# Transformer layer, attention part: a rotating accumulator bank, and row-maximum units made of every sixteenth query

## Chip, core and metric

One Trainium2 chip, one of its cores. The metric is the device time of one execution in microseconds (us): the median of the runs, for the kernel before 504.43 us.

## What is computed

A pre-norm layer on 1024 tokens of width 512 in which attention and feed-forward run side by side on the same normalized input: 32 query heads of dimension 16 share 8 key/value heads, all projections use binarized weights.

```python
def _L0_attn_ref(hidden_states, q_weight, q_scale, k_weight, k_scale, v_weight, v_scale, o_weight, o_scale):
    ...
    q = bitnet_linear(hidden_states, q_weight, q_scale)
    ...
    k = jnp.repeat(k, N_REP, axis=1)
    v = jnp.repeat(v, N_REP, axis=1)
    scores = jnp.einsum('bhqd,bhkd->bhqk', q, k) / np.sqrt(HEAD_DIM)
    attn = jax.nn.softmax(scores, axis=-1)
    out = jnp.einsum('bhqk,bhkd->bhqd', attn, v)
    out = out.transpose(0, 2, 1, 3).reshape(b, s, HIDDEN)
    return bitnet_linear(out, o_weight, o_scale)
...
xn = _layernorm(x, axis=-1)
x = x + _L0_attn_ref(xn, ...) + _L0_ffn_ref(xn, ...)
```

## The kernel before

The kernel has four stages. **Opening** (to about 60 us): loads, layer norm, transposition of x, signs of the weights, the first projections. **Feed-forward** (to 152.8 us): 28 steps F0 to F27 of gate and up matmuls, with the rest of the projections and the first 32 row units (A0 to A31) strewn between them. **Attention** (152.8 to 460 us). **Tail**: down projection, output projection, sums. The order on TensorE, VectorE and ScalarE in the second stage is written out by hand as three strings (`pe_order`, `dve_order`, `act_order`).

**Blocks and steps.** Attention runs over 16 blocks, one for each of the 8 key heads g and each half `hf` of the queries (512 of 1024). A block has 8 steps, one for each tile of 128 keys, so there are 128 steps. A block's queries are 4 heads (REP) times 512. In one step and for each of the 4 heads, TensorE makes a tile of scores [128 keys x 512 queries] into a PSUM bank, ScalarE takes its exponential into SBUF (`probs`), and TensorE multiplies that with the values of the step before (`times_values`, in two halves of 256 queries, four heads side by side in strips of 32 columns of the array) into an accumulator bank. The value matrix has ones beside it, so the accumulator also holds the sums of the softmax.

**Row units.** The exponential needs each query's maximum. For it the scores are computed a second time, the other way up: a row unit takes 128 queries as the stationary operand and all 1024 keys as the moving one (`half_rows`, twice 512 keys, into a pair of banks out of 0 to 3), and VectorE reduces the pair to one negated maximum for each query (`row_max`, a column of `nmx` [128, 16]). 16 units make a block (UNITS); they are computed two blocks ahead, two in each step. The maxima then have to become two extra rows of the queries in `qst` (a high and a low fp16 part), so that the score matmul subtracts them: for that TensorE transposes `nmx` (`transpose_max`, step "T") to [16 units, 128 queries], ScalarE copies it out of PSUM with a scale (`take_max`), GpSimd splits it into two fp16 parts (`split_max`, `shp`), and SyncE copies each part to two rows of `qst` (`load_shift`, four DMAs a block).

**Banks.** Banks 0 to 3 are those of the row units, 4, 5 and 6 go round among the score tiles, and bank 7 is always the accumulator. The transposition takes one turn of the ring of three, in step 1 of each block (`T_STEP`), between the score tiles of steps 1 and 2. At the end of a block ScalarE copies bank 7 to `osb` (`take_output`), and the first values matmul of the next block waits for that copy (`pv_free`).

**Order in a step** (`scores`): score tile 0, half a row unit, score tile 1, the other half, values part 0 of the step before, score tile 2, both halves of the second row unit, score tile 3, values part 1. A score tile is in one half of the array's rows, the row unit beside it in the other, and the two run together. From step 108 on (LATE, `late_scores`) the last 8 row units and then 56 down-projection products a tile fill the steps; the first of these steps waits for the last row maximum, since it takes bank 3 for scores.

A unit's queries as the stationary operand (`half_rows`), and the wait for the accumulator's copy (`times_values`):

```python
                                        qst[low:low + KROWS, par, hf, head, qt * P:(qt + 1) * P],
...
                        pe.wait_ge(pv_free, gp * 4 + s // TT + 2)
```

Of the kernel before, what the change touches and what calls it, by code (L numbers as in the profile page):

```python
# [13 lines left out]
P = 128  # L14
# [13 lines left out]
def layer_kernel(nc, x, wq, wk, wv, wo, wq_rows, wk_rows, wv_rows, wo_rows, sq, sk, sv, so, gate, up, down, sg, su, sd, out,  # L28
# [32 lines left out]
                "A17 F20 T0 A18 A19 F21 A20 A21 F22 A22 A23 F23 A24 A25 F24 A26 A27 F25 A28 A29 F26 A30 A31 F27 ")  # L61
# [5 lines left out]
                 "F5 F6 X4 F7 F8 F9 F10 F11 X5 F12 F13 F14 F15 F16 Y0 F17 Y1 F18 F19 F20 T0 F21 F22 F23 F24 F25 F26 "  # L67
# [6 lines left out]
    T_AT = [n for kind, n in pe_order[:pe_order.index(("T", 0))] if kind == "F"][-1]  # L74
# [3 lines left out]
    assert T_AT % 2 == 0 and len(PROJ) == 6  # L78
    assert pe_order.index(("T", 0)) > pe_order.index(("A", UNITS - 1))
# [23 lines left out]
    T_STEP = 1  # L103
    BLOCK = TT * REP
# [6 lines left out]
    def entry(j, i):  # L111

        e = j * REP + i
        e += j > T_STEP
        return e

    def score_bank(e):
        return 4 + e % 3

    T_ENTRY = (T_STEP + 1) * REP  # L120
    assert (BLOCK + 1) % 3 == 0


    LATE_SCORES = [4, 5, 6, 3]
    LATE_T = 0
    LATE_T_STEP = 3
# [5 lines left out]
    assert LATE % TT > T_STEP and ROWS_END - 1 == (2 * NG - 2) * TT + LATE_T_STEP  # L132
    assert LATE + len(QUOTAS) == NG * STEPS and sum(QUOTAS) == len(FILLS) and sum(QUOTAS[:ROWS_END - LATE]) == 2 * FT

    def t_step(block_):

        return LATE_T_STEP if block_ == 2 * NG - 2 else T_STEP

# [5 lines left out]
    def bank_of(gp, s, i):  # L144

        if gp * 2 * STEPS + s >= LATE:
            return LATE_SCORES[i]
        return score_bank(entry(s % TT, i))

    def exps_before(e):  # L150

        return e - 2 if e - 3 < T_ENTRY else max(e - 3, T_ENTRY)

# [6 lines left out]
    with ExitStack() as ctx:  # L160
# [3 lines left out]
        def sem(name):  # L164
            return ctx.enter_context(nc.semaphore(name))
# [87 lines left out]
        shp = sb("shp", [UNITS, 2, 2, P], F16)  # L253
        mxs = sb("mxs", [UNITS, P], F32)
# [74 lines left out]
        maxT_ready = sem("maxT_ready")  # L329
        max_taken = sem("max_taken")  # L330
# [169 lines left out]
        def _(pool):  # L500
# [96 lines left out]
        def _(act):  # L597
# [20 lines left out]
            def take_max(v, bank):  # L618

                act.wait_ge(maxT_ready, v + 1)  # L620
                act.wait_ge(shift_ready, v)
                nc.scalar.activation(mxs[:, :], ps[0:UNITS, bank, 0:P], ACT.Copy, scale=1.0 / LIFT).then_inc(max_taken, 1)  # L622

            splits = 0
            for kind, n in act_order:
# [51 lines left out]
                elif kind == "T":  # L677
                    take_max(0, 6)
# [17 lines left out]
            def exps(gp, s, last):  # L696
# [3 lines left out]
                if j == t_step(step // TT) + 1 and not (last and s >= STEPS + TT):  # L700
                    take_max(gp * 4 + s // TT + 1, LATE_T if step >= LATE else score_bank(T_ENTRY))
                act.wait_ge(probs_free, step + 1)
                for i, r in enumerate(ROUND):
                    act.wait_ge(scores_ready, step * REP + i + 1)
                    nc.scalar.activation(probs[:, s % 2, r, :], ps[:, bank_of(gp, s, i), :], ACT.Exp,  # L705
# [4 lines left out]
            def take_output(gp, s):  # L710
# [5 lines left out]
                nc.scalar.copy(osb[:, hf, :], ps[:, 7, :]).then_inc(pv_free, 1)  # L716
# [31 lines left out]
        def _(dve):  # L748
# [205 lines left out]
            def step_rows(gp, s, last):  # L954
# [3 lines left out]
                ga_ = gp_ * 2 + par + 1  # L958
                if step < LATE:
# [27 lines left out]
            def down_out(i):  # L987
# [5 lines left out]
                bank = FILL_BANKS[i % 2] if i < FILL else i  # L993
# [47 lines left out]
        def _(pe):  # L1041
# [73 lines left out]
            def feed_forward(w, z):  # L1115
                f, hf = w // 2, w % 2
                if z == 0:
# [6 lines left out]
                    if w == T_AT + 1:  # L1124
                        pe.wait_ge(max_taken, 1)
# [9 lines left out]

            def half_rows(par, hf, idx, b):
# [265 lines left out]
```

## Time and profile before

| | |
|---|---|
| Times of three runs | 503.80, 504.43, 505.09 us (median 504.43) |
| Profiled execution, span | 502.6 us |
| TensorE busy | 479.6 us (95%) |
| VectorE busy | 417.2 us (83%) |
| ScalarE busy | 350.3 us (70%) |
| GpSimd busy | 94.4 us (19%) |
| Granted TensorE clock | 1.000 all through (its upper level, 2.4 GHz) |

The profiled execution's own time is its span, from the first to the last instruction; the device time of a run includes what lies around it, 1.8 us at the median. "PE" is TensorE's matmuls, "PEld" its weight loads, which run beside them; DVE is VectorE, ACT ScalarE, POOL GpSimd. Matmul ends are modelled, so a PE that shows as busy is not necessarily at its peak: what counts is the distance from one start to the next.

### The profile page before, as it was taken

The page shows a single profiled execution, that of the slowest core. Times are in us where ns is not written, and L with a number is a line of the kernel's source. Part 1 is how long each engine was busy: PE and PEld are TensorE (multiplying, and loading weights), DVE is VectorE, ACT ScalarE, POOL GpSimd, SP SyncE. Part 2 cuts the span into 40 slices and gives each one's busy share as a digit, 9 for nine tenths or more (in the row PEclk, how much of TensorE's full clock was granted, in tenths as well). Part 3 has the DMA queues.
Part 4 walks back from the last instruction along what each step waited for, and adds up shares of the span by engine and source line. Part 5 has one row for each costly group of instructions (what it writes and reads, how often), then busy time and mean ns, then how long its engine had stood idle before and what let it go on. Part 6 is the DMA issues. An engine that isn't in the chain of part 4 may idle for free.

```text
span 502.6 us, 10338 instructions
## 1 busy us (share of the span) xinstructions
PE 479.6 (95%) x4186; PEld 163.0 (32%) x4186; DVE 417.2 (83%) x487; ACT 350.3 (70%) x655; POOL 94.4 (19%) x138
## 2 busy tenths in 40 slices
PE   0899999999999999999999999999999999999996
PEld 0564444434332222222222222222222233333442
DVE  6879868676778999999999999999999955223986
ACT  1853643343229999999999999999999978874000
POOL 4212334534323000000000000000000113241021
PEclk9999999999999999999999999999999999999999
DMA  8862782641103802102102211111120034452321
GB/s 260 252 123 81 159 171 38 187 91 22 23 0 42 148 23 63 40 24 65 39 25 63 40 37 49 41 53 32 41 62 24 14 96 107 110 148 79 105 82 45
DMA packets 31302, 39.02 MB, mean 78 GB/s; under 512 B 6608, under 2 KB 20816, under 8 KB 31256
## 3 DMA queue, kind: packets, MB, share of 16 engines
q1 hardware_dynamic: 22232, 27.34, 19.0%
q0 software_dynamic: 8304, 10.95, 11.8%
q8 instruction: 33, 0.54, 0.5%
q10 hardware_dynamic: 720, 0.08, 0.1%
q14 instruction: 13, 0.11, 0.1%
HBM read 33.24 MB, written 10.35 MB: 87 GB/s over the span
## 4 chain that ended last, share of the span: by engine, by line
PE 86%; ACT 8%; DVE 3%; issue 1%; DMA 1%; SPq 0%; ACTq 0%; DVEq 0%
PE ps L1301 25%; PE ps L1131 19%; PE ps L1235 12%; PE ps L1140 8%; ACT room L705 6%; PE ps L1207 5%; PE ps L1194 5%; PE ps L1110 3%; PE ps L1335 3%; PE ps L1271 2%; ACT osb L716 1%; DMA hlo<-x 1%; DVE nmx L838 1%; PE ps L1048 1%; PE ps L1102 1%
## 5 line engine op out<-in xcount | busy, mean ns | idle before, releaser
L838 DVE TENSOR_REDUCE nmx<-ps 128x1 f32<-128x1024 f32 x248 | 284.6, 1216 | 14.5 <-PE ps L1140 14.2
L705 ACT ACTIVATE room<-ps 128x512 f32<-128x512 f32 x512 | 272.4, 598 | 20.9 <-PE ps L1271 11.0
L1301 PE MATMUL ps<-room,vcur 128*32 128x256 f32 (+1 forms) x1880 | 159.1, 410 | 4.3 <-ACT osb L716 4.1
L1140 PE MATMUL ps<-kA,qst 48*128 48x512 f16 x496 | 140.4, 382 | 0.0
L1235 PE MATMUL ps<-qst,kB 50*128 50x512 f16 x432 | 132.2, 382 | 0.8 <-DVE room L937 0.5
L1131 PE MATMUL ps<-room,wf 128*128 128x512 f16 x448 | 100.6, 379 | 0.0
L1301 PEld LDWEIGHTS ps<-room,vcur 128*32 128x32 f32 x1880 | 37.1, 108 | 100.8 <-issue 55.6
L686 ACT ACTIVATE room<-ps,gsc 128x512 f32<-128x512 f32 x28 | 19.2, 687 | 61.6 <-PE ps L1131 61.6
L1131 PEld LDWEIGHTS ps<-room,wf 128*128 128x128 f16 x448 | 42.4, 98 | 55.1 <-issue 7.2
L1235 PEld LDWEIGHTS ps<-qst,kB 50*128 50x128 f16 x432 | 26.8, 93 | 89.1 <-ACT room L705 79.8
L543 POOL TENSOR_TENSOR hlo<-room,hhi 128x512 f16<-128x512 f32 x28 | 34.1, 1217 | 87.4 <-ACT hhi L616 87.4
L549 POOL TENSOR_TENSOR shp<-mxs,ones 16x128 f16<-16x128 f32 x16 | 8.1, 508 | 224.3 <-ACT mxs L622 224.3
L937 DVE SCALAR_TENSOR_TENSOR room<-ps,usc,room 128x512 f32<-128x512 f32 x28 | 20.8, 744 | 13.9 <-issue 10.0
L1140 PEld LDWEIGHTS ps<-kA,qst 48*128 48x128 f16 x496 | 26.3, 94 | 7.5 <-issue 7.5
L1194 PE MATMUL ps<-wd,hhi 128*32 128x512 f16 x224 | 22.3, 379 | 0.0
L1194 PE MATMUL ps<-wd,hlo 128*32 128x512 f16 x224 | 22.3, 379 | 0.0
L1207 PE MATMUL ps<-wd,hhi 128*128 128x512 f16 x56 | 21.2, 379 | 0.0
L1207 PE MATMUL ps<-wd,hlo 128*128 128x512 f16 x56 | 21.2, 379 | 0.0
L616 ACT CAST hhi<-room 128x512 f16<-128x512 f32 x28 | 17.1, 611 | 1.0 <-DVE room L937 1.0
L1110 PE MATMUL ps<-room,sgn 128*128 128x512 f16 x80 | 17.8, 379 | 0.0
L509 POOL TENSOR_TENSOR room<-room,parts 128x512 f32<-128x512 f32 x7 | 9.5, 1363 | 39.0 <-DVE room L994 27.4
L978 DVE TENSOR_TENSOR y<-y,ga 128x1024 f32<-128x1024 f32 (+1 forms) x5 | 5.0, 998 | 14.1 <-DMA ga<-r_scratch 14.1
(136 smaller groups left out, 320.1 us busy)
## 6 DMA issues: line engine op xcount, KB each, us to landing
qst<-q_scratch SPq DMA_DIRECT2D x32, 192.0 KB, 3.6
o_scratch<-osb SPq DMA_DIRECT2D x16, 256.0 KB, 2.3
q_scratch<-parts SPq DMA_DIRECT2D x12, 256.0 KB
hlo<-x SPq DMA_DIRECT2D x8, 256.0 KB, 6.1
parts<-x POOLq DMA_DIRECT2D x8, 256.0 KB, 3.5
wf<-gate POOLq DMA_DIRECT2D x14, 128.0 KB, 3.9
wf<-up POOLq DMA_DIRECT2D x14, 128.0 KB, 6.0
wd<-down POOLq DMA_DIRECT2D x1, 1792.0 KB, 14.3
```

The lines of the kernel that those rows point to most:

```text
L543: nc.gpsimd.tensor_tensor(hlo[:, f, hf * HALF:(hf + 1) * HALF], hb[:, w % 2, :], hhi[:, f, hf * HALF:(hf + 1) * HALF], ALU.subtract).then_ ...
L686: nc.scalar.activation(gt[:, n % 2, :], ps[:, 4 + 2 * (n % 2), :], ACT.Silu, scale=gsc[:, f:f + 1]).then_inc(gt_ready, 1)
L705: nc.scalar.activation(probs[:, s % 2, r, :], ps[:, bank_of(gp, s, i), :], ACT.Exp, scale=gam_reg[par][r]).then_inc(scores_free, 1)
L838: nc.vector.tensor_reduce(nmx[:, hf, idx:idx + 1], bank_pair(idx % 2), AX.X, ALU.max, negate=True).then_inc(rows_free, 1)
L937: nc.vector.scalar_tensor_tensor(out=hb[:, n % 2, :], in0=ps[:, 5 + 2 * (n % 2), :], scalar=usc[:, f:f + 1], in1=gt[:, n % 2, :], op0=ALU. ...
L1110: mm = nc.tensor.matmul(ps[:, 2 * (n % 2) + hf, :], sgn[:, c, c0:c0 + P], xs[:, c, hf * HALF:(hf + 1) * HALF], start=(c == 0 and xs is xhi ...
L1131: mm = nc.tensor.matmul(ps[:, 4 + 2 * (w % 2) + z, :], wf[:, f % WF_BUFS, z, c * P:(c + 1) * P], xs[:, c, hf * HALF:(hf + 1) * HALF], star ...
L1140: return nc.tensor.matmul(ps[:, 2 * (idx % 2) + b, :], qst[low:low + KROWS, par, hf, head, qt * P:(qt + 1) * P], kA[low:low + KROWS, par, ...
L1194: mm = nc.tensor.matmul(ps[32 * c:32 * c + 32, FILL_BANKS[i % 2], :], (hhi, hlo)[part][:, f, lo:lo + 32], wd[:, f, :], start=(f == 0 and p ...
L1207: mm = nc.tensor.matmul(ps[:, i, :], (hhi, hlo)[part][:, f, i * P:(i + 1) * P], wd[:, f, :], start=(f == 0 and part == 0), stop=(f == FT - ...
L1235: nc.tensor.matmul(ps[:, score_bank(e), :], kB[low:low + SROWS, par, kt % (TT // 2) * P:(kt % (TT // 2) + 1) * P], qst[low:low + SROWS, pa ...
L1301: mm = nc.tensor.matmul(ps[32 * r:32 * r + 32, 7, of], vcur[:, par, key_tile(r, j), :], probs[:, s % 2, r, of], start=(j == 0 and part == ...
```

## The change

It has two parts. **The accumulator bank changes at each block**: at step 1 of a block, before score tile 2, the bank next in the ring becomes the block's accumulator, and the accumulator of the block before joins the ring in its place. So the first values matmul of a block no longer waits for ScalarE's copy; score tile 2 of that step does. **A row unit takes every sixteenth query** (all 4 heads, 32 queries of each, starting at query u for unit u) instead of 128 neighbours of one head. Then `nmx` [128, 16], read row by row, has the 2048 queries in their order, and needs no transposition. The T steps of TensorE and the `take_max` steps of ScalarE are gone; GpSimd scales `nmx` itself (twice, once to fp32 and once to fp16) and subtracts, and the DMAs read 128 partitions of 32 bytes in place of 16 of 256. VectorE gets one wait at the start of each block, that the maxima which it overwrites have been split.

```diff
-                "A17 F20 T0 A18 A19 F21 A20 A21 F22 A22 A23 F23 A24 A25 F24 A26 A27 F25 A28 A29 F26 A30 A31 F27 ")
+                "A17 F20 A18 A19 F21 A20 A21 F22 A22 A23 F23 A24 A25 F24 A26 A27 F25 A28 A29 F26 A30 A31 F27 ")
...
-                 "F5 F6 X4 F7 F8 F9 F10 F11 X5 F12 F13 F14 F15 F16 Y0 F17 Y1 F18 F19 F20 T0 F21 F22 F23 F24 F25 F26 "
+                 "F5 F6 X4 F7 F8 F9 F10 F11 X5 F12 F13 F14 F15 F16 Y0 F17 Y1 F18 F19 F20 F21 F22 F23 F24 F25 F26 "
...
+    SPLIT_AT = 20
+    ring, spare = [4, 5, 6], 7
+    score_banks, score_after, value_banks = {}, {}, [7]
+    last_exp, last_copy = {}, {}
+
+    for step in range(LATE):
+        block_, j = step // TT, step % TT
+        for i in range(REP):
+            if i == 2 and j == 1 and block_ >= 1:
+                value_banks.append(ring.pop(0))
+                ring.insert(0, spare)
+                last_copy[spare] = block_
+                spare = value_banks[-1]
+            bank = ring.pop(0)
+            ring.append(bank)
+            score_banks[step, i] = bank
+            score_after[step, i] = last_exp.get(bank, 0), last_copy.pop(bank, 0)
+            last_exp[bank] = step * REP + i + 1
...
-        shp = sb("shp", [UNITS, 2, 2, P], F16)
-        mxs = sb("mxs", [UNITS, P], F32)
+        shp = sb("shp", [P, 2, 2, UNITS], F16)
+        mxs = sb("mxs", [P, UNITS], F32)
...
             def split_max(v, hf):
-                pool.wait_ge(max_taken, v + 1)
-                nc.gpsimd.tensor_tensor(shp[:, hf, 0, :], mxs[:, :], ones[0:UNITS, :], ALU.mult).then_inc(shift_step, 1)
-                pool.wait_ge(shift_step, v + 1)
+                pool.wait_ge(rows_free, 2 + (v + 1) * UNITS)
+                pool.wait_ge(shift_ready, v)
+                nc.gpsimd.tensor_scalar(mxs[:, :], nmx[:, hf, :], 1.0 / LIFT, 1.0, ALU.mult, ALU.mult).then_inc(shift_step, 1)
+                nc.gpsimd.tensor_scalar(shp[:, hf, 0, :], nmx[:, hf, :], 1.0 / LIFT, 1.0, ALU.mult,
+                                        ALU.mult).then_inc(shift_step, 1)
+                pool.wait_ge(shift_step, 2 * (v + 1))
                 nc.gpsimd.tensor_tensor(shp[:, hf, 1, :], mxs[:, :], shp[:, hf, 0, :], ALU.subtract).then_inc(shift_ready, 1)
...
-                if w == T_AT + 1:
+                if w == SPLIT_AT:
                     split_max(0, 0)
...
-                nc.scalar.activation(mxs[:, :], ps[0:UNITS, bank, 0:P], ACT.Copy, scale=1.0 / LIFT).then_inc(max_taken, 1)
...
-                nc.scalar.copy(osb[:, hf, :], ps[:, 7, :]).then_inc(pv_free, 1)
+                nc.scalar.copy(osb[:, hf, :], ps[:, value_banks[v], :]).then_inc(pv_free, 1)
...
+                if j == 0 and step < LATE:
+                    dve.wait_ge(shift_ready, ga_ * 2 + hf - 1)
...
+            def unit_queries(low, par, hf, idx):
...
+                return qst[low:low + KROWS, par, hf].rearrange("p h (i u) -> p u h i", u=UNITS)[:, idx]
...
-                                        qst[low:low + KROWS, par, hf, head, qt * P:(qt + 1) * P],
+                return nc.tensor.matmul(ps[:, 2 * (idx % 2) + b, :], unit_queries(low, par, hf, idx),
...
-                nc.tensor.transpose(ps[0:UNITS, bank, 0:P], nmx[:, hf, :], ident[:, :]).then_inc(maxT_ready, 1)
...
-                    pe.wait_ge(scores_free, block_ * BLOCK + exps_before(e) + 3)
-                    if e - 3 == T_ENTRY:
-                        pe.wait_ge(max_taken, block_ + 2)
+                    exps_done, copies_done = score_after[step, i]
+                    pe.wait_ge(scores_free, 3 + exps_done)
+                    if copies_done:
+                        pe.wait_ge(pv_free, 2 + copies_done)
...
-                if j == T_STEP:
-                    pe.wait_ge(scores_free, block_ * BLOCK + exps_before(T_ENTRY) + 3)
-                    transpose_max(block_ + 1, 1 - hf, score_bank(T_ENTRY))
...
-                        pe.wait_ge(pv_free, gp * 4 + s // TT + 2)
+                        if step_ >= LATE:
+                            pe.wait_ge(pv_free, step_ // TT + 2)
```

The transposition of step 115 and the wait for `max_taken` ahead of one output projection go in the same way, and the late steps and the down projection take their banks from the new lists.

## Rows read from the trace of the kernel before

**Rows 1.** The page: span, busiest engine, shares of the chain that ended last.
```profile
span 502.6 us, 10338 instructions
PE 479.6 (95%) x4186; PEld 163.0 (32%) x4186; DVE 417.2 (83%) x487; ACT 350.3 (70%) x655; POOL 94.4 (19%) x138
PE 86%; ACT 8%; DVE 3%; issue 1%; DMA 1%; SPq 0%; ACTq 0%; DVEq 0%
```

**Rows 2.** Groups by line, VectorE's maxima: busy us, mean ns | idle before.
```profile
L838 DVE TENSOR_REDUCE nmx<-ps 128x1 f32<-128x1024 f32 x248 | 284.6, 1216 | 14.5 <-PE ps L1140 14.2
```

**Rows 3.** Timeline of VectorE in attention: start us, length us, merged instructions [idle before].
```profile
153.61 5.00 DVE L838 TENSOR_REDUCE nmx<-ps 128x1 f32<-128x1024 f32 x4
159.01 18.21 DVE L838 TENSOR_REDUCE nmx<-ps 128x1 f32<-128x1024 f32 x16 [0.40 <-PE ps L1140]
...
306.11 18.22 DVE L838 TENSOR_REDUCE nmx<-ps 128x1 f32<-128x1024 f32 x16 [0.15 <-PE ps L1140]
324.48 18.21 DVE L838 TENSOR_REDUCE nmx<-ps 128x1 f32<-128x1024 f32 x16 [0.15 <-PE ps L1140]
...
397.96 4.62 DVE L838 TENSOR_REDUCE nmx<-ps 128x1 f32<-128x1024 f32 x4 [0.15 <-PE ps L1140]
```

**Rows 4.** Timeline of ScalarE: one block, then a late step.
```profile
302.88 0.59 ACT L716 COPY osb<-ps 128x512 f32<-128x512 f32 x1
...
305.90 15.46 ACT L705 ACTIVATE room<-ps 128x512 f32<-128x512 f32 x28
...
408.14 2.06 ACT L705 ACTIVATE room<-ps 128x512 f32<-128x512 f32 x4 [0.55 <-PE ps L1271]
```

**Rows 5.** Timeline of TensorE: steps 1 and 2 of that block, then plain steps.
```profile
302.59 0.39 PE L1235 MATMUL ps<-qst,kB 50*128 50x512 f16 x1
...
303.52 0.64 PE L1301 MATMUL ps<-room,vcur 128*32 128x256 f32 x8 [0.32 <-ACT osb L716]
...
305.20 0.28 PE L1151 MATMUL ps<-ident,nmx 128*16 128x128 f32 x1
...
305.41 0.39 PE L1235 MATMUL ps<-qst,kB 50*128 50x512 f16 x1
...
307.65 0.39 PE L1235 MATMUL ps<-qst,kB 50*128 50x512 f16 x1
...
308.19 0.64 PE L1301 MATMUL ps<-room,vcur 128*32 128x256 f32 x8
...
309.87 0.39 PE L1235 MATMUL ps<-qst,kB 50*128 50x512 f16 x1
```

**Rows 6.** Groups by line and form, weight loads: rows*columns of the array, mean ns.
```profile
L1301 PEld LDWEIGHTS ps<-room,vcur 128*32 128x32 f32 x1880 | 37.1, 108 | 100.8 <-issue 55.6 <-ACT room L705 34.0 <-ACT osb L716 11.0
L1140 PEld LDWEIGHTS ps<-kA,qst 48*128 48x128 f16 x496 | 26.3, 94 | 7.5 <-issue 7.5
L1194 PEld LDWEIGHTS ps<-wd,hhi 128*32 128x32 f16 x224 | 6.6, 97 | 9.6 <-issue 6.1
L1080 PEld LDWEIGHTS ps<-power,pick 128*128 128x128 f32 x8 | 1.0, 192 | 0.0
```

**Rows 7.** Timeline of TensorE in feed-forward, around the first transposition.
```profile
123.89 0.27 PE L1151 MATMUL ps<-ident,nmx 128*16 128x128 f32 x1
124.10 0.61 PE L1140 MATMUL ps<-kA,qst 48*128 48x512 f16 x4
```

**Rows 8.** Timeline of TensorE in the late steps: 108, then 115 and 116.
```profile
402.64 0.60 PE L1278 MATMUL ps<-kA,qst 48*128 48x512 f16 x2
...
422.52 0.28 PE L1151 MATMUL ps<-ident,nmx 128*16 128x128 f32 x1
422.73 0.61 PE L1271 MATMUL ps<-qst,kB 50*128 50x512 f16 x4
```

**Rows 9.** The shift's way to the queries: GpSimd's split, the DMA issues (KB, us to landing).
```profile
L549 POOL TENSOR_TENSOR shp<-mxs,ones 16x128 f16<-16x128 f32 x16 | 8.1, 508 | 224.3 <-ACT mxs L622 224.3
qst<-shp SPq DMA_DIRECT2D x64, 4.0 KB, 1.8
```

More of the change, by code:

```diff
@@ L77, in layer_kernel @@
     SUM_AT = [n for kind, n in pe_order[pe_order.index(("S", 1)):] if kind == "A"][0]
-    assert T_AT % 2 == 0 and len(PROJ) == 6
-    assert pe_order.index(("T", 0)) > pe_order.index(("A", UNITS - 1))
+    SPLIT_AT = 20
+    assert len(PROJ) == 6
+    assert dve_order.index(("F", SPLIT_AT)) > dve_order.index(("A", UNITS - 1))
     assert [n for kind, n in pe_order if kind in "FU"] == list(range(FU))
@@ L142, in fills_of, with bank_of @@
         return FILLS[done:done + QUOTAS[step - LATE]]
-    def bank_of(gp, s, i):
-        if gp * 2 * STEPS + s >= LATE:
+    ring, spare = [4, 5, 6], 7
[14 more added lines that the diff above has]
+            last_exp[bank] = step * REP + i + 1
+    value_banks += value_banks[-1:] * (2 * NG - len(value_banks))
+    LATE_SCORES = sorted({4, 5, 6, 7} - {value_banks[-1]}) + [3]
+    D_BANK = [0, 1, 2, 3] + LATE_SCORES[0:3] + value_banks[-1:]
+    def bank_of(step, i):
+        if step >= LATE:
             return LATE_SCORES[i]
-        return score_bank(entry(s % TT, i))
-    def exps_before(e):
-        return e - 2 if e - 3 < T_ENTRY else max(e - 3, T_ENTRY)
+        return score_banks[step, i]
     def at(gp, s):
@@ L699, in exps @@
                 step = gp * (2 * STEPS) + s
-                if j == t_step(step // TT) + 1 and not (last and s >= STEPS + TT):
-                    take_max(gp * 4 + s // TT + 1, LATE_T if step >= LATE else score_bank(T_ENTRY))
                 act.wait_ge(probs_free, step + 1)
@@ L704, in exps @@
                     act.wait_ge(scores_ready, step * REP + i + 1)
[L705 removed]
+                    nc.scalar.activation(probs[:, s % 2, r, :], ps[:, bank_of(step, i), :], ACT.Exp,
                                          scale=gam_reg[par][r]).then_inc(scores_free, 1)
@@ L992, in down_out @@
                     dve.wait_ge(down_ready, i - FILL + 1)
-                bank = FILL_BANKS[i % 2] if i < FILL else i
+                bank = FILL_BANKS[i % 2] if i < FILL else D_BANK[i]
                 nc.vector.tensor_tensor(ffn[i], ps[:, bank, :], dsb[:, :], ALU.mult).then_inc(ff_ready, 1)
@@ L1206, in down_proj @@
                         pe.wait_ge(pv_free, 2 + 2 * NG)
-                mm = nc.tensor.matmul(ps[:, i, :], (hhi, hlo)[part][:, f, i * P:(i + 1) * P], wd[:, f, :],
+                mm = nc.tensor.matmul(ps[:, D_BANK[i], :], (hhi, hlo)[part][:, f, i * P:(i + 1) * P], wd[:, f, :],
                                       start=(f == 0 and part == 0), stop=(f == FT - 1 and part == 1))
@@ L1214, in scores @@
                 gp_, par, hf, j = at(gp, s)
-                block_ = gp * 4 + s // TT
+                step = gp * (2 * STEPS) + s
+                block_ = step // TT
                 if j == 0:
@@ L1277, in late_scores @@
                     for b in range(2):
-                        mm = nc.tensor.matmul(ps[:, b, :],
-                                              qst[b * HI:b * HI + KROWS, 1, 1, unit % UNITS // (HALF // P),
-                                                  unit % (HALF // P) * P:(unit % (HALF // P) + 1) * P],
+                        mm = nc.tensor.matmul(ps[:, b, :], unit_queries(b * HI, 1, 1, unit % UNITS),
                                               kA[b * HI:b * HI + KROWS, 1, :], start=True, stop=True)
@@ L1285, in late_scores @@
                     down_strips(*fill)
-                if step == ROWS_END - 1:
-                    transpose_max(2 * NG - 1, 1, LATE_T)
             def times_values(gp, s, part, cut):
@@ L1311, in _ @@
                 for i in range(REP):
-                    last_use[bank_of(step // (2 * STEPS), step % (2 * STEPS), i)] = step * REP + i + 1
+                    last_use[bank_of(step, i)] = step * REP + i + 1
             scores(0, 0, opening=True)
```

42 lines of the change are left out of this document (4 added, 38 removed).

## The prediction, made before the changed kernel had run

> **What bounds the kernel now.** I read the page first. TensorE is busy 95% of the span and makes 86% of the chain that ended last [rows 1]. That share is an average over stages, and matmul ends are modelled, so I went on to the timelines of attention and looked at starts, engine by engine, for what repeats.
>
> What repeats is a block of 18.37 us: VectorE's runs of 16 maxima start at 306.11 and 324.48 [rows 3]. Inside it TensorE takes 2.22 us for a plain step (307.65 to 309.87), but 2.82 us for step 1 (302.59 to 305.41) and 2.24 us for step 2 (305.41 to 307.65) [rows 5]. Five other steps are at 2.22, and so is step 0. A block is thus 8 x 2.22 = 17.74 us of steps and 0.63 us of boundary. The boundary has two visible causes. First, the values matmuls of step 1 start 0.93 us after the step (302.59 to 303.52), with ScalarE's copy of the accumulator named as the releaser; in a plain step it is 0.54 us (307.65 to 308.19) [rows 5]. That is 0.38 us. Second, the transposition takes the place of 0.21 us in TensorE's stream (305.20 to 305.41) [rows 5]. Step 2 adds 0.03 us. ScalarE is not what bounds a plain step: 28 exponentials in 15.46 us are 0.55 us each [rows 4], and it waits in them for score tiles.
>
> The second thing to see is how little VectorE is behind. Its 16 maxima take 16.99 us from the first start to the last (18.21 us less one of 1.216) [rows 2, 3], so they are 1.133 us apart, and 16 of them need 18.13 us. **Of the 18.37 us of a block VectorE is idle or late for only 0.24 us**, once, at the boundary, with TensorE's row unit as releaser [rows 3]. In a plain step it needs 2.27 us against TensorE's 2.22: it falls behind by 0.05 us a step and catches up at the boundary. The last maximum of attention proper is the fourth of the run that starts at 397.96, so it starts at 401.36 and ends at 402.58 [rows 3]. The first late step's row unit starts at 402.64, right behind it [rows 8]. Attention before the late steps is therefore paced as a whole by VectorE's 216 maxima, from 153.61 on, plus what they wait.
>
> **Part 1, the accumulator bank.** Removed: the wait of 0.38 us at each of 13 block starts ahead of step 108. Added: score tile 2 of step 1 waits for the copy. The copy ends at 303.47 (302.88 plus 0.59) [rows 4]. Without its stall TensorE would be at score tile 2 half a step, 1.11 us, after 302.59, at 303.70, so this wait is over by then. Behind it in the queue would stand both halves of the second row unit, for which VectorE waits, and score tile 3; it is covered by 0.2 us, and if that cover were gone each block would lose what is missing, at most the 0.38 us of now. ScalarE still copies, and that costs it about one exponential's time (0.5 us). It has 2.27 - 4 x 0.49 = 0.3 us to spare in each step (0.49 us is the distance of exponentials which don't wait: four in a late step take 2.06 us, less one of 0.59, over three [rows 4]), so it is level again after two steps, and the scores that wait for its banks may come 0.1 us late. I take 0.1 us of boundary for TensorE. The late blocks keep the old wait.
>
> **Part 2, no transposition.** Removed from TensorE: 16 transpositions of 0.21 us, 14 of them in blocks 0 to 13, one in feed-forward (123.89 to 124.10) [rows 7], one in step 115 (422.52 to 422.73) [rows 8]. The latter two stages run TensorE without gaps of another cause, so they bring 0.2 us each. Removed from ScalarE: the 16 `take_max` copies out of PSUM, which stood ahead of the exponentials of step 2. Moved to GpSimd: three operations over [128, 16] where two over [16, 128] took 0.51 us and about as much again [rows 9]. It waited 224 us in total for its input [rows 9], so even 3 x 0.51 us are covered; in feed-forward they stand ahead of one fp16 low part, for which GpSimd otherwise waits idle. The four DMAs land 1.8 us after issue [rows 9]. With 128 pieces of 32 bytes for 16 of 256 no row shows their time; even four times as long is nothing beside the 18 us until the block that needs them. The tightest is the last: its maximum is there at 422.5 [rows 8], and four late steps, none shorter than 2.22 us, stand before its block; split, issue and landing take 1.5 + 2.4 + 1.8 us. VectorE's new wait, for a split made more than a block earlier, is satisfied when it comes, and so should cost nothing. No row has it on VectorE; the nearest are ScalarE's exponentials, of which the first of each step waits twice: at 0.55 us for 0.49 they lose 0.06 us each, 0.24 us a step, all of it to the second wait at worst [rows 4]. In 13 blocks that is 0 to 3.1 us. I take 0, as that loss has another cause, the wait for score tiles.
>
> **Part 3, what the new units cost TensorE.** This is the edit that no row shows. The moving side of a row unit is unchanged. The stationary side is now read at every sixteenth fp16 element, 32 bytes apart; no load in this kernel has a step. Nearest rows: a load of 128 fp16 columns takes 94 ns, no more than one of 32 fp16 columns (97 ns), while 128 fp32 columns take 192 ns and 32 take 108 [rows 6]. So the fp16 load gets its 128 columns in the time of 32, and a column costs (192 - 108) / 96 = 0.9 ns where they come one after the other. Call the lengthening d. At the low end d is 0 (a gain is excluded, since nothing of the load gets smaller). The next value is the 32 column times doubled, d = 0.028 us. The third is the load that loses its fourfold reading, d = 0.084 us. Further out both at once: 0.2 us. It isn't hidden: the first row unit of each half step is loaded when the array changes over from the values matmuls, together with the score tile's own load, and everything in the half step follows it. So a step costs 2.22 + 2d. The 18 groups of row units in feed-forward and the 8 of the late steps cost d each.
>
> The Trainium skill has two rules here. TensorE: Matmul & The Clock Gate, section Weight-path perf modes, says that the fast weight load reads its four chunks of 32 columns "packed or strided", up to a column step of 1,024 elements; by that the step of 16 keeps it, and d is near 0. Advanced Engine Details and Errata, section SBUF Cachelines, says that a line is 16 bytes and that reads which hit another line each time are penalised; that speaks against this change. No row of this trace settles either. I take d = 0, since it is nearest to the rows, where the load's time hardly goes with the number of columns.
>
> **The sum.** With d = 0 TensorE's block would be 17.74 + 0.1 = 17.84 us, under VectorE's 18.13 us. **VectorE becomes the bound**, TensorE waits for it in every step, and a block saves 18.37 - 18.13 = 0.24 us, not the 0.5 us that TensorE alone gains. The margin holds: a released row unit's second half starts 0.22 us after the first and ends 0.39 us later [rows 5], so it is ready some 0.65 us after its banks come free, and it is wanted after 1.13 us. 13 blocks give 3.1 us. Block 0 has more idle time, 0.40 us ahead of its fifth maximum [rows 3], of which the transposition and the ring's turn explain 0.36 us. One run is 0.14 us longer than its neighbours (the one from 214.12, by a hesitation of TensorE), which TensorE's new slack covers. Together 3.6 us, and the late steps start so much earlier, since they hang on the last maximum. With the two of 0.2 us: **4.0 us**. Span 502.6 to 498.6 us; the median of the runs lies 1.8 us above the profiled span, so 504.4 to **500.4 us**. The floor is VectorE without any idle time from 153.61 on: 215 x 1.133 = 243.6 us against 247.75 us now, 4.15 us, with the 0.4 us and 0.2 us more for what the late steps might gain: 499.5 us.
>
> **Rivals.** (a) **The load at a step is slower by a line's penalty**, d = 0.028 us. TensorE's block is 17.84 + 16 x 0.028 = 18.29 us, now above VectorE's. From d = 0.017 us on (where 17.84 + 16d passes 18.13) the whole comes to 242d - 7.9 us (216 half steps and 26 groups; 13.5 blocks of 0.53 us, block 0 and the two transpositions on the other side). At 0.028 that is -1.1 us: 503.3 us. For it: each column lies in a line of its own. Against: a column needs 0.9 ns today, slow enough that a second access might fit in. By the errata page's rule this would be the result.
> (b) **Slower than before: the load loses its fourfold reading**, d = 0.084 us. It decides from d = 0.033 us on, where 242d passes 7.9 us, in the half steps, at the change from values to scores. +12.4 us: 516.8 us. For it: only packed loads of 128 columns are seen at 94 ns. Against: the queries of one unit lie at one even step over all four heads (32 x 16 = 512 is a head's length), so the operand is as regular as before. With d = 0.2 us it would be 545 us.
> (c) **The change doesn't do what it says**: the wait for the copy stays in another place (score tile 2) and ScalarE's copy holds the ring. A block then keeps 0.38 us and loses only the transposition's part; TensorE's 18.12 us meets VectorE's 18.13, so the result is the same 500.4 to 501 us. It needs no chance of its own; it only takes away the slack.
> (d) VectorE pays the new wait in full: up to 503.5 us, inside my range.
>
> **How the numbers follow.** d from 0 to 0.017 us with (c) and (d): 0.54, 500.4 us, own range 499.3 to 501.6. Rival (a), d from 0.017 to 0.033: 0.24, 501 to 504.5. Rival (b) and what lies around it: 0.22, of which 0.06 up to 507 us (d about 0.045). A measurement of this kernel can tell 0.3%, 1.5 us, from no change. Faster by more than that is all of the first case and a fourth of (a): 0.60. Within it: the rest of (a) and a little of (b): 0.20. Slower: 0.20. The range leaves out the farther part of (b), 0.16, and a little below: 499.0 to 507.0 us.
>
> **What would show it.** Right: the weight loads of the row units stay at 94 ns; VectorE's maxima run 1.13 us apart over whole blocks, a block is 18.13 us; TensorE's steps become 2.27 us with VectorE as the releaser of row units; values matmuls of step 1 start 0.54 us after their step. Wrong: loads over 110 ns and plain steps over 2.27 us with no wait for VectorE (then d is what the loads say); a step 1 that still stands out, with score tile 2 waiting for the copy; gaps between VectorE's maxima, or a late block start that waits for the shift.

## The result and the profile after

The changed kernel takes 508.81 us (median of 10 runs, 506.78 to 512.66), the kernel before 504.43 us beside it (10 runs, 503.66 to 507.82). The ratio is 1.0079 with a 95% interval of 1.005 to 1.0108: **slower by 0.8%**, where 500.4 us and faster was forecast and the range ended at 507.0. The profiled execution is the fastest of the ten, 504.7 us of span against 502.6 us.

The page and its groups by line, the lines that answer to [rows 1], [rows 2] and [rows 6]:

```profile
span 504.7 us, 10296 instructions
PE 485.8 (96%) x4170; PEld 173.1 (34%) x4170; DVE 420.8 (83%) x487; ACT 349.7 (69%) x639; POOL 90.6 (18%) x154
PE 94%; DVE 3%; DMA 1%; ACT 1%; issue 1%; SPq 0%; ACTq 0%; DVEq 0%
L824 DVE TENSOR_REDUCE nmx<-ps 128x1 f32<-128x1024 f32 x248 | 288.2, 1218 | 13.1 <-PE ps L1129 12.5
L1217 PEld LDWEIGHTS ps<-qst,kB 50*128 50x128 f16 x432 | 35.4, 104 | 91.4 <-ACT room L691 78.2
L1129 PEld LDWEIGHTS ps<-kA,qst 48*128 48x128 f16 x496 | 37.9, 144 | 7.6 <-issue 7.6
L543 POOL TENSOR_SCALAR mxs<-nmx 128x16 f32<-128x16 f32 x16 | 3.7, 234 | 218.3 <-DVE nmx L824 218.1
```

The load of a row unit takes 144 ns where it took 94. Those of the score tiles, unchanged, rise from 93 to 104, since in attention every second one now takes 115 to 121 ns; in the variant below in which they no longer stand behind such a load they are all near 92 again. TensorE's share of the chain has gone from 86% to 94%. GpSimd's three new operations take 0.20 to 0.23 us each.

VectorE's, ScalarE's and TensorE's timelines, as in [rows 3], [rows 4] and [rows 5]:

```profile
153.68 250.51 DVE L824 TENSOR_REDUCE nmx<-ps 128x1 f32<-128x1024 f32 x216
404.89 1.22 DVE L953 TENSOR_REDUCE nmx<-ps 128x1 f32<-128x1024 f32 x1 [0.71 <-PE ps L1257]
```
```profile
304.09 0.59 ACT L702 COPY osb<-ps 128x512 f32<-128x512 f32 x1
304.55 18.17 ACT L691 ACTIVATE room<-ps 128x512 f32<-128x512 f32 x32
322.61 0.59 ACT L702 COPY osb<-ps 128x512 f32<-128x512 f32 x1
```
```profile
303.85 0.39 PE L1217 MATMUL ps<-qst,kB 50*128 50x512 f16 x1
...
304.44 0.64 PE L1277 MATMUL ps<-room,vcur 128*32 128x256 f32 x8
...
306.18 0.39 PE L1217 MATMUL ps<-qst,kB 50*128 50x512 f16 x1
...
310.82 0.39 PE L1217 MATMUL ps<-qst,kB 50*128 50x512 f16 x1
...
311.98 0.39 PE L1217 MATMUL ps<-qst,kB 50*128 50x512 f16 x1
...
313.14 0.39 PE L1217 MATMUL ps<-qst,kB 50*128 50x512 f16 x1
```

The boundary is gone as intended. Step 1 takes 2.33 us (303.85 to 306.18), its values matmuls start 0.59 us after it, as in every step of this kernel, and ScalarE's copy stands among 32 exponentials with no gap. But a plain step takes 2.31 us instead of 2.22: step 2 to step 5 of that block, 306.18 to 313.14, is 2.32 us a step, and a half step (310.82 to 311.98) 1.16 us for 1.11. A block is 18.52 us (322.61 less 304.09) for 18.37. The merged line of 216 maxima hides that: (250.51 - 1.22) / 215 is 1.160 us from start to start, VectorE waiting a little each time for its row unit.

The second loss is at the last block, which starts 3.57 us after the step before it, not 3.04 (TensorE's timeline; then SyncE's, with the shift's DMA issues; then the time to landing of all 64 of them, after, and before):

```profile
433.25 0.61 PE L1250 MATMUL ps<-qst,kB 50*128 50x512 f16 x4
...
436.82 0.61 PE L1250 MATMUL ps<-qst,kB 50*128 50x512 f16 x4 [0.45 <-issue]
```
```profile
427.13 2.41 SPq L398 DMA_DIRECT2D qst<-shp  x4
```
```profile
DMA to landing us min/median/max: 1.9/2.1/7.8
```
```profile
DMA to landing us min/median/max: 1.6/1.8/6.8
```

**Where the time went**, from the starts of row units, steps and blocks in both timelines: feed-forward from its first row maximum to the first score tile 84.69 us for 84.01 (+0.7); attention up to step 108 250.57 us for 248.94 (+1.6); from there to the last block 33.39 us for 33.19 (+0.2: the stall of 0.52 less the transposition, 0.22, and an easier entry, 0.10); the last block and the tail 67.9 us for 67.7 (+0.2). The opening was 0.6 us shorter; it differs by up to 1.9 us between executions of all kernels here (first row maximum at 67.7 to 69.6 us) and says nothing about the change. That makes the +2.1 us of the two spans, and less than the +4.4 us of the medians. 0.3 us of the rest lies outside the span: in every execution on record with both numbers the time is 1.7 to 1.8 us above the span for the kernel before and for the rotation alone, which keep the transposition, and 2.0 to 2.1 us for all kernels without it. Why is open. The stall and the clock, further on, vary between executions and take their part; the clocks of these ten executions of the kernel before aren't on record, so the rest of the +4.4 us isn't split.

### The profile page after: what moved, and what is told of

Read it like the earlier page. It is cut to its first block, busy times and chain, and to the rows that moved or that the text cites. A ratio compares the mean times of both kernels' runs of the same rounds, so it can differ in the third digit from the quotient of the medians.

```text
span 504.7 us, 10296 instructions
## 1 busy us (share of the span) xinstructions
PE 485.8 (96%) x4170; PEld 173.1 (34%) x4170; DVE 420.8 (83%) x487; ACT 349.7 (69%) x639; POOL 90.6 (18%) x154
## 4 chain that ended last, share of the span: by engine, by line
PE 94%; DVE 3%; DMA 1%; ACT 1%; issue 1%; SPq 0%; ACTq 0%; DVEq 0%
PE ps L1277 28%; PE ps L1117 19%; PE ps L1217 16%; PE ps L1129 11%; PE ps L1188 5%; PE ps L1175 5%; PE ps L1098 3%; PE ps L1311 3%; PE ps L1250 2%; DMA hlo<-x 1%; DVE stats L750 1%; DVE room L772 1%; PE ps L1090 1%; DVE room L777 0%; ACT room L691 0%
## 5 line engine op out<-in xcount | busy, mean ns | idle before, releaser
L824 DVE TENSOR_REDUCE nmx<-ps 128x1 f32<-128x1024 f32 x248 | 288.2, 1218 | 13.1 <-PE ps L1129 12.5
L1217 PE MATMUL ps<-qst,kB 50*128 50x512 f16 x432 | 141.9, 382 | 0.7 <-DVE room L923 0.4
L1217 PEld LDWEIGHTS ps<-qst,kB 50*128 50x128 f16 x432 | 35.4, 104 | 91.4 <-ACT room L691 78.2
L543 POOL TENSOR_SCALAR mxs<-nmx 128x16 f32<-128x16 f32 x16 | 3.7, 234 | 218.3 <-DVE nmx L824 218.1
L1129 PEld LDWEIGHTS ps<-kA,qst 48*128 48x128 f16 x496 | 37.9, 144 | 7.6 <-issue 7.6
L953 DVE TENSOR_REDUCE nmx<-ps 128x1 f32<-128x1024 f32 x8 | 9.8, 1222 | 8.2 <-PE ps L1257 8.2
```

What stands on the lines that cost most here:

```text
L824: nc.vector.tensor_reduce(nmx[:, hf, idx:idx + 1], bank_pair(idx % 2), AX.X, ALU.max, negate=True).then_inc(rows_free, 1)
L1129: return nc.tensor.matmul(ps[:, 2 * (idx % 2) + b, :], unit_queries(low, par, hf, idx), kA[low:low + KROWS, par, :], start=True, stop=True)
L1217: nc.tensor.matmul(ps[:, bank_of(step, i), :], kB[low:low + SROWS, par, kt % (TT // 2) * P:(kt % (TT // 2) + 1) * P], qst[low:low + SROWS, ...
```

## The experiments

**Neighbouring queries again.** Whether the load is the whole loss is told by giving only the operand back.

```diff
-                return qst[low:low + KROWS, par, hf].rearrange("p h (i u) -> p u h i", u=UNITS)[:, idx]
+                head, qt = idx // (HALF // P), idx % (HALF // P)
+                return qst[low:low + KROWS, par, hf, head, qt * P:(qt + 1) * P]
...
-                    nc.vector.tensor_scalar(gam[:, :], spread, SCALE / Q_GAIN, None, ALU.mult).then_inc(gam_ready, 1)
+                    nc.vector.tensor_scalar(gam[:, :], spread, SCALE / Q_GAIN / 256.0, None, ALU.mult).then_inc(gam_ready, 1)
```

> The changed kernel, but each row unit takes 128 neighbouring queries of one head again. The maxima then go to the wrong queries; so that no exponential overflows, the scale inside the exponential is divided by 256. All instructions are otherwise those of the changed kernel. Theory A (the load at a step of 16 elements costs 0.045 us in each half step of TensorE and is the whole loss): loads of the row units back from 144 to 94 ns, TensorE no longer the bound, VectorE's maxima 1.13 us apart, a block 18.13 us instead of 18.52, median about 501 us (500.4 forecast for a free load, plus the 0.5 us stall at the last block). Theory B (the loss comes from the rotating bank or from the wait on VectorE): the block stays at 18.5 us and the median near 508.

Measured: 502.09 us, with 505.81 us for the kernel before on that chip, ratio 0.9931 (0.9907 to 0.9956); span 499.7 us. Its loads, TensorE and VectorE:

```profile
L1130 PEld LDWEIGHTS ps<-kA,qst 48*128 48x128 f16 x496 | 24.8, 93 | 7.6 <-issue 7.6
```
```profile
299.77 0.39 PE L1218 MATMUL ps<-qst,kB 50*128 50x512 f16 x1
299.80 0.58 PE L1130 MATMUL ps<-kA,qst 48*128 48x512 f16 x2
...
302.03 0.39 PE L1218 MATMUL ps<-qst,kB 50*128 50x512 f16 x1
302.06 0.58 PE L1130 MATMUL ps<-kA,qst 48*128 48x512 f16 x2
```
```profile
299.64 20.46 DVE L824 TENSOR_REDUCE nmx<-ps 128x1 f32<-128x1024 f32 x18
```

Theory A holds. (20.46 - 1.22) / 17 is 1.132 us for a maximum: VectorE is never late, and all blocks from the third on take 18.10 us (the second 18.01). TensorE's step is now 2.26 us, VectorE's pace, and the row unit starts 0.03 us behind its score tile, released by VectorE, instead of with it. This is the mechanism of the forecast, seen alone, with a free load. Theory B falls: the rotating bank, VectorE's new wait and GpSimd's work cost nothing that shows. In feed-forward, from the first row maximum to the first score tile, it is 83.90 us, where the kernel before takes 84.01 and every kernel here with all units at a step of 16 takes 84.7: 0.8 us for 18 groups of row units, 0.044 us each. In the late steps the load costs nothing that shows: steps 112 to 115 take 2.40, 2.40, 2.44 and 2.40 us in this run and in the changed kernel alike.

**Each part alone.** The units without the rotation, and the rotation without the units (the transposition takes its turn in the ring as before):

```diff
-            if i == 2 and j == 1 and block_ >= 1:
-                value_banks.append(ring.pop(0))
...
-                        if step_ >= LATE:
-                            pe.wait_ge(pv_free, step_ // TT + 2)
+                        pe.wait_ge(pv_free, step_ // TT + 2)
```

> Only the second part of the change: units of every sixteenth query, no transposition, but the accumulator stays in bank 7 and each block's first values matmul waits for the copy. Theory A: steps of 2.31 us and on top the 0.38 us of that wait in 13 blocks, so a block of 18.52 + 0.3 = 18.8 us and a median some 4 us above the changed kernel, 512 us. Theory B (the bank rotation costs, not the units): a block of at most 18.5 us, 508 us or less.

```diff
+        if j == T_STEP:
+            bank = ring.pop(0)
+            ring.append(bank)
+            turn_bank[block_], turn_after[block_] = bank, last_exp.get(bank, 0)
+            last_take[bank] = block_ + 2
...
+                        if step_ >= LATE:
+                            pe.wait_ge(pv_free, step_ // TT + 2)
```

> Only the first part of the change: the accumulator bank changes at each block, the row units stay as before and the maxima are still transposed. Theory A: TensorE's block is 17.74 + 0.21 for the transposition + 0.1 = 18.0 to 18.1 us, just under VectorE's 18.13, so VectorE sets the pace: block 18.13 us, 3 to 3.5 us less than before, median 501.2. Theory B: no gain or a loss, 504 us or more.

Measured: the units alone 511.88 us, ratio 1.0138 (1.0098 to 1.0178), all blocks from the second on 18.78 us; the rotation alone 503.49 us, ratio 0.9963 (0.9927 to 0.9999), blocks of 18.21 us. So the rotation was worth 0.16 us a block without the units (18.37 to 18.21) and 0.26 us with them (18.78 to 18.52). The units cost 0.41 us a block on their own: 16 half steps of 0.045 us are 0.72, less a remainder of 0.31 for the transposition and its copy. Theory A of the first run holds (18.8 us and 512 us expected). Of the second neither holds in full: it is 2.3 us under the kernel before on that chip, 505.81 us, where 3 to 3.5 were expected, with an interval that ends just under 1. 18.21 us is more than the 18.13 expected: steps 1 and 2 take 2.53 and 2.38 us for 2.22. The transposition, ScalarE's two copies and the ring all meet there; which of them holds the steps up wasn't tested. VectorE catches up its lag and waits 0.1 us.

**What the load costs by its step.** One kernel with eight steps, one for each pair of units in a block:

```diff
+                if idx // 2 == 1:
+                    return nc.tensor.matmul(to, flat[:, 0:2 * P:2], keys, start=True, stop=True)
...
+                return nc.tensor.matmul(to, flat[:, 0:16 * P:16], keys, start=True, stop=True)
```

> The changed kernel with row units whose 128 query columns lie at a step of 1, 2, 3, 4, 6, 8, 12 or 16 fp16 elements (2 to 32 bytes), one step for each of the eight pairs of units in a block. The maxima belong to other queries, and the scale in the exponential is divided by 256. Theory A1 (a penalty for each 16-byte line that is entered anew): the load's time grows with the step from 94 ns and stops growing at a step of 8 (16 bytes), where each column has a line of its own. Theory A2 (the load reads two neighbouring fp16 elements at once and loses that with any step): the whole 45 ns are there from a step of 2 on. Theory A3 (conflicts of certain steps): 8 and 16 are slow, 3, 6 and 12 are not.

Its weight loads by line (one execution), duration in ns min/median/max; from the top the steps are 1, 2, 3, 4, 6, 8, 12 and 16 elements:

```profile
L1132 PEld LDWEIGHTS ps<-kA,qst x64: 92/93/96, 67.3 to 392.7; 48*128 48x128 f16 x64
L1134 PEld LDWEIGHTS ps<-kA,qst x64: 92/94/112, 71.2 to 395.0; 48*128 48x128 f16 x64
L1136 PEld LDWEIGHTS ps<-kA,qst x64: 99/101/113, 75.3 to 397.3; 48*128 48x128 f16 x64
L1138 PEld LDWEIGHTS ps<-kA,qst x64: 107/109/127, 90.2 to 399.6; 48*128 48x128 f16 x64
L1140 PEld LDWEIGHTS ps<-kA,qst x60: 121/124/144, 97.8 to 383.6; 48*128 48x128 f16 x60
L1142 PEld LDWEIGHTS ps<-kA,qst x60: 138/142/163, 101.9 to 385.9; 48*128 48x128 f16 x60
L1144 PEld LDWEIGHTS ps<-kA,qst x60: 135/141/158, 106.0 to 388.2; 48*128 48x128 f16 x60
L1145 PEld LDWEIGHTS ps<-kA,qst x60: 137/141/163, 110.2 to 390.5; 48*128 48x128 f16 x60
```

Theory A1 holds in its shape: the time grows up to a step of 8 elements and then stands still; only at a step of 2 it doesn't grow yet. A step of 8 is 16 bytes. Counted in 16-byte pieces touched by the 128 columns, it is 93 ns at 16 pieces, 94 at 32, 101 at 48, 109 at 64, 124 at 96 and 142 at 128, and no more than that however far apart they lie: above some 32 pieces each further one costs 0.5 ns. A2 (all of it at a step of 2) and A3 (12 is as slow as 8 and 16) fall.

What that does to TensorE's steps stands in the same profile, since each step of a block has its own step of the columns. The starts of the steps with the load at 1 and 2, then at 4, 6, 8 and 12 elements:

```profile
190.62 0.39 PE L1232 MATMUL ps<-qst,kB 50*128 50x512 f16 x1
...
192.84 0.39 PE L1232 MATMUL ps<-qst,kB 50*128 50x512 f16 x1
...
197.43 0.39 PE L1232 MATMUL ps<-qst,kB 50*128 50x512 f16 x1
...
199.68 0.39 PE L1232 MATMUL ps<-qst,kB 50*128 50x512 f16 x1
...
201.95 0.39 PE L1232 MATMUL ps<-qst,kB 50*128 50x512 f16 x1
...
204.27 0.39 PE L1232 MATMUL ps<-qst,kB 50*128 50x512 f16 x1
```

With the load at 93 ns the step takes 2.22 us (190.62 to 192.84), at 109 ns 2.25, at 124 ns 2.27, at 142 ns 2.32. A step has two half steps and so two such loads, and 2.22 us plus twice what the load takes above 93 ns gives 2.25, 2.28 and 2.32: the lengthening is exposed in full.

The flat end is the rule of Advanced Engine Details and Errata (section SBUF Cachelines) in the Trainium skill, a penalty for reads that enter a new 16-byte line each time, and the trace agrees with that. The same section of the Trainium skill asks for at least two hits on a line; here that isn't enough, for with two columns in each line (a step of 4) the load already takes 109 ns. The rule of the other page, TensorE: Matmul & The Clock Gate (section Weight-path perf modes) in the Trainium skill, that the fast weight load also takes strided chunks, isn't contradicted: the load at a step takes 142 ns, not the 192 ns of the 128 fp32 columns in [rows 6]. But it gives no time for a step.

**The load behind score matmuls.** If the load at a step only costs because it stands where the array changes over, another order hides it:

```diff
-                    if i < REP - 1:
-                        if i % 2 == 0:
-                            pe.wait_ge(rows_free, (gp_ * 2 + par + 1) * (2 * UNITS) + hf * UNITS + idx + 1)
-                        mm = half_rows(1 - par, hf, idx, 1 - half)
...
+                    if i % 2 == 1:
+                        idx = 2 * j + i // 2
+                        pe.wait_ge(rows_free, (gp_ * 2 + par + 1) * (2 * UNITS) + hf * UNITS + idx + 1)
+                        half_rows(1 - par, hf, idx, 1 - half)
+                        half_rows(1 - par, hf, idx, half).then_inc(rows_ready, 1)
```

> The changed kernel with another order in TensorE's half step: both score tiles first, then both halves of the row unit, then the values. The loads at a step of 16 (137 to 148 ns) then come behind score matmuls in the same array rows (213 ns of streaming) and not behind values matmuls. Theory A, and the load is hidden there: plain steps of TensorE at or under 2.27 us, VectorE sets the pace, block 18.13 us, median about 501 us. Rival: the load holds up the array wherever it stands: steps stay 2.31 us, median 508. Second rival: ScalarE's ring of three banks gets too tight, since score tile 3 wants the bank of tile 0 0.22 us earlier: steps over 2.31 us.

Measured: 505.87 us, ratio 1.0018 (0.9991 to 1.0045), span 502.6 us. Plain steps are 2.25 us, so the load is hidden. But the block is 18.24 us, not 18.10, for both theories had a part: step 1 takes 2.51 us. ScalarE's copy delays the exponential of score tile 0, and score tile 3 wants its bank; with the row unit now behind tile 3, VectorE waits too. The second rival was right for one step in eight. The median is 4.9 us above the 501 us expected, and level with the kernel before. In the profiles attention up to step 108 gains 1.9 us on the kernel before, but feed-forward, whose order is unchanged, loses 0.7 us, the last block starts after a step of 3.76 us for 3.04, the last block and the tail take 0.4 us more, and 0.3 us come outside the span.

**The last shift.** GpSimd holds back the next loads until the shift is there:

```diff
             split_max(2 * NG - 1, 1)
+            pool.wait_ge(shift_loaded[1][1], 64 * NP)
             for u in range(2, QT - 1):
```

> The changed kernel, but GpSimd's queue waits until the last shift has landed before it issues the loads of the third slice of the output. In the changed kernel's profile the step before the last block took 3.57 us for 3.04, with the last pieces of the shift landing among the 4 KB packets of these loads. Theory C (the last shift is late because its 512 pieces of 32 bytes queue behind these loads): that step is 3.05 us again and the kernel 0.5 to 1.6 us faster than the changed kernel, with less spread from run to run. Rival: the shift is late because GpSimd splits late: the step stays at 3.5 us or more.

> The changed kernel once more, beside the two variants on the same chip, for its spread. Block of 18.52 us and late stall as in its profile. Theory C: the step before the last block varies between executions (3.0 to 4.6 us), and the time varies with it.

Measured on the same chip: the changed kernel 509.32 us (507.04 to 510.22), ratio 1.0076 (1.0052 to 1.01); with the wait 507.66 us (506.95 to 508.77), ratio 1.0048 (1.0031 to 1.0065). The step before the last block without and with the wait (TensorE's timelines of the changed kernel's second profile and of the variant):

```profile
432.79 0.61 PE L1250 MATMUL ps<-qst,kB 50*128 50x512 f16 x4
...
437.05 0.61 PE L1250 MATMUL ps<-qst,kB 50*128 50x512 f16 x4 [1.14 <-issue]
```
```profile
433.46 0.60 PE L1251 MATMUL ps<-qst,kB 50*128 50x512 f16 x4
...
436.51 0.60 PE L1251 MATMUL ps<-qst,kB 50*128 50x512 f16 x4
```

The landing of the last four DMAs, in the changed kernel's first profile and in the variant:

```profile
DMA to landing us min/median/max: 3.0/3.8/7.8
```
```profile
DMA to landing us min/median/max: 2.4/3.4/3.7
```

Theory C holds for the cause: 4.26 us become 3.05, the slowest landing 3.7 us. The rival falls: the four issues come no earlier (from 427.35 us on, for 427.13). The median falls by 1.7 us and the spread from 3.2 to 1.8 us, but the two intervals overlap, so the size in the time is less certain than the stall itself. In the six profiles without the wait that have no transposition the step took 3.57, 3.64, 3.76, 3.94, 4.26 and 4.62 us, in the two with it 3.04 and 3.05, as in the kernel before and in the rotation alone. The pieces of the shift, now eight times as many and 32 bytes each, move among the 4 KB packets of the loads, to 435.6 us; with the loads held back the last one moves at 431.5. The loads beside them are worth about 4 us of landing (7.8 to 3.7). The smaller pieces come with about 1 us more (6.8 us in the kernel before and 7.2 with the rotation alone, among the same loads, 7.8 to 8.8 in the six); no run changes the pieces alone. Part of the gain goes again: with the loads late, the sixth step of the last block takes 3.33 us, and 3.27 in the run below, for 3.05.

**Both mended.** Score tiles first, except in the second half of step 1, and the wait for the last shift:

```diff
+                    early = j == 1 and i == 2
+                    if early or (i % 2 == 1 and not (j == 1 and i == 3)):
+                        first = 1 - half
+                        pe.wait_ge(rows_free, (gp_ * 2 + par + 1) * (2 * UNITS) + hf * UNITS + idx + 1)
+                        half_rows(1 - par, hf, idx, first)
+                        half_rows(1 - par, hf, idx, 1 - first).then_inc(rows_ready, 1)
```

> The changed kernel with score tiles first in each half step, except the second half of step 1, where score tile 3 would wait for a bank that the copy holds up (2.51 us for 2.25 in the run with score tiles first everywhere); and with the last shift landing before the loads of the third slice. Theory A: all steps of TensorE under VectorE's 2.26 us, block 18.10 us as with neighbouring queries, 0.14 us less in each of 13 blocks than with score tiles first everywhere and no stall at the last block: 2.4 us less than that, some 1.5 to 2.5 us under the kernel before. Rival: step 1 keeps 0.2 us in another wait, block 18.2 us.

Measured: 502.71 us (501.31 to 504.55) beside 505.45 us for the kernel before, ratio **0.9943** (0.9922 to 0.9964). It beats both kernels, 2.7 us under the kernel before and 6.6 us under the changed one. Its loads still take 144 ns; in attention they are out of the way, while feed-forward still pays its 0.7 us for them (84.68 us for 84.01):

```profile
L1130 PEld LDWEIGHTS ps<-kA,qst 48*128 48x128 f16 x496 | 36.1, 144 | 7.6 <-issue 7.6
```
```profile
163.64 236.52 DVE L825 TENSOR_REDUCE nmx<-ps 128x1 f32<-128x1024 f32 x209 [0.76 <-PE ps L1130]
```

(236.52 - 1.22) / 208 is 1.131 us: VectorE runs without a gap, 16 maxima in 18.10 us. TensorE's blocks from the second on take 18.08 us, and VectorE falls 0.02 us behind in each.

## Why the prediction was wrong, point by point

**What bounded the kernel before: right.** VectorE was idle for 0.24 us of a block, and with the load free the block is 18.10 us where 18.13 was worked out. The gain stops there.

**The accumulator bank: right in direction, and right in size with part 2.** The values matmuls of step 1 start on time, and score tile 2 doesn't wait for the copy. TensorE's block in the changed kernel is 8 x 2.31 + 0.04 us; the 0.1 us of boundary was a little too much.

**The transposition: right for TensorE's steps, half of it in feed-forward.** Step 115 takes 2.40 us for 2.62, but feed-forward without it and with a free load only 83.90 us for 84.01: 0.1 us, not 0.2. ScalarE and GpSimd took their parts as described.

**The load: the step that failed.** The prediction took d = 0, "since it is nearest to the rows". It is 0.045 us in TensorE's half step (plain steps of 2.31 us for 2.22, loads of 137 to 148 ns for 94), between rival (a) with 0.028 and rival (b) with 0.084. The mechanism was described as it is: exposed where the array changes over from the values matmuls, once in each half step and in each group of units of feed-forward, decisive from d = 0.033 us on. Only the 8 groups of the late steps, which were to cost d each, cost nothing. What failed was the size, 0 for 0.045 us. Rival (a)'s size was wrong by its own working: it doubled the time of 32 columns that are read abreast, at 0.9 ns each, where the runs show a cost for each 16-byte piece of all 128 columns, 96 pieces above 32 at 0.5 ns. The formula 242d - 7.9 gives +3.0 us at 0.045. From the first row maximum to the last block the profiles show +2.5, and +2.0 without the stall of 0.5: the formula has 0.5 us too much in the late steps and 0.5 to 0.6 in attention, whose block is 18.52 us and not 17.84 + 16 x 0.045 = 18.56. The variant without the stall is 2.2 us above the kernel before in its median, 0.3 of them outside the span. The chance of 0.54 for a load that is free leaned on rows in which all columns are neighbours; they could say nothing about a step.

**The last shift: the second step that failed.** "The tightest is the last ... split, issue and landing take 1.5 + 2.4 + 1.8 us." The term for the landing was mis-sized: 1.8 us was the median of all 64 DMAs, and what counts is the last of the last four, which share the DMA engines with the loads of the output's third slice. These are the four in the kernel before:

```profile
L405 SPq DMA_DIRECT2D qst<-shp x4: 509/590/593, 425.7 to 427.5; - x4
DMA to landing us min/median/max: 3.0/3.3/6.8
```

The last is issued at 427.5 us and lands 6.8 us later, at 434.3, and the last block starts at 434.91: there were 0.6 us to spare, where the prediction's terms leave at least 3.2 (four steps of 2.22 less 5.7). The way to the first issue was short as well: it comes 3.2 us after the last maximum, not 1.5. In the changed kernel the issues come no later against TensorE's steps, but the last one, at 428.9 us, takes 7.8 us, to 436.7, and the block, due at 436.3, starts at 436.82. Such steps are 0.5 to 1.6 us too long in the six profiles. On the second chip the medians rise by 2.2 us without the stall and by 1.7 more with it; the two make up the 3.9 us between 505.45 and 509.32 by subtraction, which checks neither.

**The rivals.** (c) and (d), the copy's wait moved and VectorE's wait paid, did not occur. Rival (b) named the side and the place, at a size (516.8 us) that wasn't reached. The range was too narrow above since between d = 0.028 and 0.084 it stopped at 0.045 and held nothing back for the shift. The floor's own sum, 4.15 + 0.4 + 0.2 us below 504.4, is 499.7 us and not 499.5; nothing hangs on it.

## What to carry to other kernels

A stationary operand read at a step is no free re-indexing: count the 16-byte pieces that its columns touch, and put such a load behind matmuls in the same array rows and not first after a change from the values' tiling, where it was exposed in full here. When an edit takes a step out of a chain, work out first which engine is next (here VectorE, 0.24 us a block behind), since that caps the gain, while a cost on the old bound has no such cap. For a small transfer with a deadline take the landing of that very one in the trace, beside whatever shares the DMA engines then, and not the median of all.

## What the runs showed of the hardware

- The load of 128 fp16 columns: 93 ns packed, 94 ns at a step of 4 bytes, 109 ns at 8 bytes, 142 ns at 16 bytes, and flat beyond, to 32 bytes.
- Where the array changes over from the values matmuls, this lengthening went into TensorE's step in full, 0.10 us for two loads of 142 ns; behind score matmuls it didn't show (steps of 2.25 us).
- The last four DMAs of the shift landed after up to 7.8 to 8.8 us beside loads of 4 KB packets (six profiles), and after up to 3.7 and 4.0 us without them (two).
- At the start of attention TensorE's granted clock fell to its lower level (1.2 GHz) for a few us in some executions and not in others. TensorE had come from feed-forward's unbroken matmuls (busy 14.55 of the 15 us before) into the first steps, in which it waits for VectorE and ScalarE. In the mended kernel's profile (columns: stretch, us, busy us of each engine with counts, granted clock, DMA share, GB/s)

```profile
155.00:165.00 10.00, 9.49 (x64) 1.99 (x63) 7.10 (x7) 7.21 (x15) 3.19 (x6) 0.66 0.46 63
165.00:400.00 235.00, 235.00 (x2504) 70.98 (x2496) 235.00 (x208) 225.57 (x430) 11.85 (x47) 1.00 0.22 49
```

  the clock is 0.66 on the mean of ten us, which is 6.8 us at the lower level, and block 0 takes 21.5 us, where it takes 18.9 us with the full clock in the variant with score tiles first. In the changed kernel's profile the same stretch is at 1.00:

```profile
155.00:165.00 10.00, 9.71 (x99) 2.89 (x99) 9.70 (x9) 9.72 (x20) 3.19 (x6) 1.00 0.59 81
```

  The kernel before has executions of both kinds too (mean clocks of 0.992 to 1.000 at 508.3 to 503.3 us), so this is part of the spread of all kernels here. The difference stays without it: of the executions of the second chip at 0.999 or more, the kernel before has a median of 505.0 us (7 of them) and the changed kernel 509.7 (4).
